# A gated two-layer transformer kernel on one Trainium2 core: block loads two blocks ahead, constants spread over later units, the next stage's first tiles loaded early

## The reference, cut to what matters

```python
x = x + tanh(g_xattn[0]) * L0_xattn(layernorm(x), ctx)       # first stage
xq   = act_fake_quant(layernorm(x))                          # one scale for the tensor
gate = xq @ weight_fake_quant(w_gate).T                      # 512 -> 1408
up   = xq @ weight_fake_quant(w_up).T
h    = act_fake_quant(silu(gate) * up)                       # scale: the largest |h| of all
x = x + tanh(g_ffn[0]) * h @ weight_fake_quant(w_down).T     # gate, up: second stage; down: third
x = x + tanh(g_xattn[1]) * L1_xattn(layernorm(x), ctx)       # third stage
x = x + tanh(g_ffn[1]) * L1_ffn(layernorm(x))                # ternary weights, third stage
```

## Time and profile before

| | |
|---|---|
| median of 3 runs | 1998.06 us (1998.03 to 2000.37) |
| the profiled execution's own time | 1998.16 us |
| its span in the trace | 1996.4 us |
| granted TensorE clock, mean | 0.972 of full speed |
| busy share: PE, DVE, ACT, POOL | 80%, 87%, 74%, 31% |
| stage two (first row product to `b_done`) | about 971 to 1176 us |
| stage three | about 1176 us to the end |

### The profile page before, as it was taken

One profiled execution on the slowest core, in us unless ns is written; L12 is line 12 of the kernel. 1 busy time (PEld: TensorE's weight loads), 2 busy tenths in 40 slices (PEclk: granted clock), 3 DMA queues, 4 the chain that ended last, 5 costly groups with the idle time before them and its releaser, 6 DMA issues.

```text
span 1996.4 us, 24448 instructions
## 1 busy us (share of the span) xinstructions
PE 1607.0 (80%) x9510; PEld 719.2 (36%) x9510; DVE 1744.6 (87%) x2619; ACT 1485.4 (74%) x1098; POOL 616.0 (31%) x480
## 2 busy tenths in 40 slices
PE   6868965697658966785598969999999987888886
PEld 3212211132112211231243435666666643334432
DVE  6899998999999988898577767999999669999997
ACT  4899999999999999999253745555454357767771
POOL 1000000000000000000161226666666545887882
PEclk9999999999999999999799989999999988999999
DMA  5000200020000010000485753333332111432312
GB/s 198 1 8 30 69 11 1 22 74 22 1 1 1 22 53 1 1 11 1 157 315 215 257 174 123 106 101 108 112 107 84 43 35 32 72 55 76 63 43 74
DMA packets 116709, 143.65 MB, mean 72 GB/s; under 512 B 25326, under 2 KB 74606, under 8 KB 116210
## 3 DMA queue, kind: packets, MB, share of 16 engines
q1 hardware_dynamic: 116594, 142.10, 22.8%
HBM read 87.55 MB, written 50.33 MB: 69 GB/s over the span
## 4 chain that ended last, share of the span: by engine, by line
ACT 42%; PE 29%; DVE 18%; issue 4%; DMA 3%; POOL 3%; SPq 0%; DVEq 0%; POOLq 0%; ACTq 0%
ACT unit L514 39%; PE psum L1645 5%; PE psum L1679 5%; PE psum L1631 3%; DVE hmax_parts L1427 3%; DVE psum L1416 3%; PE psum L1009 3%; PE psum L1015 3%; DVE unit L423 2%; PE psum L1655 2%; DMA xblk<-xnT_scratch 2%; PE psum L1672 2%; PE psum L1664 1%; POOL hidden L1835 1%; PE psum L547 1%
## 5 line engine op out<-in xcount | busy, mean ns | idle before, releaser
L514 ACT ACTIVATE unit<-unit 128x4096 f32<-128x4096 f32 x244 | 857.5, 3615 | 0.5 <-DVE unit L423 0.3
L423 DVE TENSOR_SCALAR unit<-feat_proj,text_proj 128x1024 f32<-128x1024 f32 x976 | 667.3, 746 | 67.2 <-PE psum L639 65.4
L639 PE MATMUL psum<-unit,w_pad 128*32 128x512 f32 x3904 | 474.4, 604 | 234.1 <-ACT unit L514 234.1
L639 PEld LDWEIGHTS psum<-unit,w_pad 128*32 128x32 f32 x3904 | 102.5, 110 | 556.7 <-ACT unit L514 398.2
L680 POOL TENSOR_SCALAR red<-red 128x8 f32<-128x8 f32 x4 | 2.0, 509 | 531.5 <-DVE red L321 531.5
L1818 POOL TENSOR_TENSOR h<-h,arow 128x512 f32<-128x512 f32 x104 | 135.7, 1318 | 72.1 <-ACT h L1580 71.7
L1697 PE MATMUL psum<-xq_block,w_q 128*128 128x512 bf16 x512 | 125.7, 391 | 25.4 <-ACT hidden L1599 21.0
L680 POOL TENSOR_SCALAR rstd<-mv 128x8 f32<-128x8 f32 (+1 forms) x5 | 1.7, 336 | 411.4 <-DVE mv L216 411.4
L547 PE MATMUL psum<-xnT,W_sb 128*128 128x512 f32 x256 | 125.2, 617 | 2.1 <-ACT xnT L465 2.1
L1587 ACT ACTIVATE psum<-h,conv_b_sb,conv_w_sb 128x512 f32<-128x512 f32 x112 | 86.2, 779 | 53.4 <-POOL h L1818 46.6
L1732 PE MATMUL psum<-w_q,hidden_q 128*128 128x512 fp8e4 x448 | 101.3, 379 | 21.1 <-ACT hidden_q L1610 10.8
(11 more groups left out here) (255 smaller groups left out, 2756.8 us busy)
## 6 DMA issues: line engine op xcount, KB each, us to landing
h_scratch<-h SPq DMA_DIRECT2D x44, 512.0 KB, 3.5
hin<-h_scratch SPq DMA_DIRECT2D x32, 704.0 KB, 4.7
xin<-in_x SPq DMA_DIRECT2D x8, 1024.0 KB, 6.7
tern_in<-in_w1T SPq DMA_DIRECT2D x16, 512.0 KB, 5.4
tern_in<-in_w2T SPq DMA_DIRECT2D x16, 512.0 KB, 5.4
x<-in_x SPq DMA_DIRECT2D x16, 512.0 KB, 3.6
x_scratch<-x SPq DMA_DIRECT2D x32, 256.0 KB, 2.0
x3in<-x_scratch SPq DMA_DIRECT2D x31, 256.0 KB, 3.1
```

Source lines behind the costliest of these rows:

```text
L423: ins = ve.tensor_scalar(units[:, n % 3, k, :], FP[:, bi % 2, k, :], TP[:, k, n:n + 1], None, ALU.add)
L514: ac.activation(units[:, n % 3], units[:, n % 3], ACT.Tanh).then_inc(unit_tanh, 1)
L639: mm = te.matmul(psum[k * TG:(k + 1) * TG, 3 + 2 * grp + half, :], w_pad[:, k, TG - 1 - tt:2 * TG - 1 - tt], units[:, n % 3, k, half * BAN ...
```

## The change

It changes when SyncE issues four kinds of load in stage two, the order of TensorE's first six half products, when VectorE makes the mask, and what opens stage three:

- The half blocks of the third and fourth block are loaded right behind the unit that rounds the buffer's old content two blocks earlier, in units 5 and 9 of block `o` for block `o + 2` (units 5, 9, 16 and 20, in place of 13, 17, 24 and 28).
- The seven constants are loaded one by one in units 18 to 24, and the mask and `bo_row` are made in unit 28.
- In unit 36 SyncE loads the first two tiles of `hin` and the first group of `x`, ahead of the store of that unit. `hin` and `x2` were moved in SBUF for this (behind `scores`).
- TensorE starts with the products of the first half of the first block: gate 0, up 0, gate 1, then the same three for the second half.
- ScalarE goes into stage three on `hscale_step` 5 (the reciprocal of the scale) and waits for `b_done` only before the second tile. VectorE scales `bq` and copies the keys behind the clip of the second tile (slot 315) in place of ahead of everything.

```diff
+    PREFETCH_SLOT = 36
+    CONST_SLOT, MASK_SLOT = 18, 28
...
-            if n == 10:
+            if n == MASK_SLOT:
                 V.wait_ge(const_c_loaded, NCONST_C)
...
+        def product(pair, w, n, half):
+            o, i = divmod(n, NI)
+            T.wait_ge(xq_step, 3 * (2 * o + half + 1))
+            for k in range(KC):
+                mm = te.matmul(pair[:, half, :], w[:, k, i * P:(i + 1) * P],
+                               xqT[:, o % 2, k, half * BLK:(half + 1) * BLK], start=(k == 0), stop=(k == KC - 1))
+            return mm
+
+        for half in range(2):
+            mm = product(gate_pair(0), wgT, 0, half)
...
+            mm = product(up_pair(0), wuT, 0, half)
...
+            mm = product(gate_pair(1), wgT, 1, half)
...
         for n in range(NH):
             o, i = divmod(n, NI)
...
+            if n > 1:
+                T.wait_ge(h_done, 2 * (n - 2) + 1)
+                product(gate_pair(n), wgT, n, 0)
+                product(gate_pair(n), wgT, n, 1).then_inc(gate_mm, 1)
+            if n > 0:
+                T.wait_ge(silu_done, n)
+                product(up_pair(n), wuT, n, 0)
+                product(up_pair(n), wuT, n, 1).then_inc(up_mm, 1)
...
             for half in range(2):
-                if 1 <= o < NB - 1 and i == ROUND_SLOT[half] - 2:
-                    load_block(o + 1, half)
+                if o + 2 < NB and i == ROUND_SLOT[half] + 1:
+                    load_block(o + 2, half)
             for r in range(2, KC):
                 if n == NI * (r - 1):
                     load_down(r)
+            if CONST_SLOT <= n < CONST_SLOT + len(consts):
+                sp.dma_start(*consts[n - CONST_SLOT]).then_inc(const_c_loaded, 16)
+            if n == PREFETCH_SLOT:
+                S.wait_ge(xq_step, 6 * NB)
+                stored = NI * (ORDER.index(0) + 1) - 1
+                for q in range(HR):
+                    S.wait_ge(h_stored[q], 16 * ((stored - q) // HR + 1))
+                for t in range(2):
+                    sp.dma_start(hin[:, t], h_dram[0][:, :, t * P:(t + 1) * P]).then_inc(hin_loaded[t], 16)
+                sp.dma_start(x2[:, 0:TPG, :], x[0:GRP, :].rearrange("(i p) d -> p i d", p=P)).then_inc(x2_loaded[0], 16)
             S.wait_ge(h_done, 2 * n + 1)
...
+    KEYS_AT = HQ2[1] + 1
...
+            if q == KEYS_AT:
+                ve.tensor_scalar(bq_s[:, :], bq_sb[:, :], INV_SQRT_HD, None, ALU.mult).then_inc(kd_copied, 1)
+                V.wait_ge(edges_done, 1)
...
     def scalar_C():
-        A.wait_ge(b_done, 1)
+        A.wait_ge(hscale_step, 5)
...
             for g, i, t in at1(q, SHIFT):
+                if t == 1:
+                    A.wait_ge(b_done, 1)
```

More of the change, by code:

```diff
@@ L1002, in tensor_B @@
         T.wait_ge(kv_copied, KC + NB)
+        def product(pair, w, n, half):
[7 more added lines that the diff above has]
+            mm = product(gate_pair(0), wgT, 0, half)
+            if half == 1:
+                mm.then_inc(gate_mm, 1)
+            mm = product(up_pair(0), wuT, 0, half)
+            if half == 1:
+                mm.then_inc(up_mm, 1)
+            mm = product(gate_pair(1), wgT, 1, half)
+            if half == 1:
+                mm.then_inc(gate_mm, 1)
         for n in range(NH):
             o, i = divmod(n, NI)
[L1005 to L1017, removed]
+            if n > 1:
[6 more added lines that the diff above has]
+                product(up_pair(n), wuT, n, 1).then_inc(up_mm, 1)
             for half in range(2):
@@ L1083, in sync_B @@
         load_down(1)
[L1084 to L1087, removed]
+        consts = ((bq_sb[:, :], bq), (bo_row[:, :], bo.broadcast_to([P, D])), (cw_sb[:, :, :], conv_w),
+                  (cb_sb[:, :], conv_b), (km_u8[:, :, :], kmask.rearrange("(t p) k -> p t k", p=P)),
+                  (wq_sb[:, :, :], WqT), (wo_sb[:, :, :], WoT))
         for n in range(NH):
@@ L1126, in flamingo @@
     pc = ExitStack()
-    hin = sb("hin", [P, 2, NI, P], stack=pc)
     hq = sb("hq", [P, 2, NI, P], BF16, stack=pc)
@@ L1132, in flamingo @@
     qT = sb("qT", [P, KC, GRP], stack=pc)
+    sc = sb("scores", [P, 2, HEADS, TXT], stack=pc)
+    hin = sb("hin", [P, 2, NI, P], stack=pc)
     X2R = 8
@@ L1136, in flamingo @@
     kbd = sb("k_diag", [P, NB, KC, 2 * TXT], stack=pc)
-    sc = sb("scores", [P, 2, HEADS, TXT], stack=pc)
     pT = sb("probT", [P, 2, PAIRS, P], stack=pc)
@@ L1318, in vector_C @@
     def vector_C():
[L1319 to L1325, removed]
         steps = [0]
@@ L1347, in attention @@
                 ve.tensor_scalar(hq[:, i], hq[:, i], -QMAX - 1.0, None, ALU.max).then_inc(hq_done, 1)
+            if q == KEYS_AT:
+                ve.tensor_scalar(bq_s[:, :], bq_sb[:, :], INV_SQRT_HD, None, ALU.mult).then_inc(kd_copied, 1)
+                V.wait_ge(edges_done, 1)
+                for h in range(HPC):
+                    rows = slice(h * HD, (h + 1) * HD)
+                    ins = ve.tensor_copy(kbd[rows, :, :, (h % 2) * TXT:(h % 2 + 1) * TXT],
+                                         kT[rows, :, :].rearrange("p m (b k) -> p b m k", b=NB))
+                ins.then_inc(kd_copied, 1)
             for g, i, t in at1(q, DSC):
@@ L1858, in attention @@
             for g, i, t in at1(q, X2LOAD):
-                load_x(g)
+                if g > 0:
+                    load_x(g)
             for g, i, t in at1(q, HQ2):
@@ L1915, in feed_forward @@
                     load_rows(t + 2)
-        for t in range(2):
-            load_tile(t)
         for q in range(min(0, X2LOAD[0]), QEND):
```

## The result

The changed kernel takes 1984.44 us (median of four runs, 1981.02 to 1985.88), beside 1998.32 us for the kernel before (1998.03 to 2000.37). The ratio is 0.9924, with a 95% interval of 0.9911 to 0.9936: 14 us less. The profiled execution was the fastest of the four, 1981.02 us with a span of 1979.2.

A forecast was written before the change was run, and what follows sets the result against it. The prediction took TensorE as the bound in stage three and, where undisturbed, in stage two, whose gaps could be won; its terms summed to -20.3 us, 1977.8 us from the median of 1998.06, range 1971 to 1985.

The forecast's parts named there:

- my own forecast: Whole kernel: the case that the summed terms hold, 1974 to 1982 us, chance 0.55.
- the tighter engines: Rival: VectorE or ScalarE becomes the bound of stage two, 1982 to 1991 us, chance 0.17.
- (a): Start of stage two: first products by halves let up 1 start earlier, -2.7 us.
- (b): Unit 16: the earlier load removes VectorE's wait in unit 13 and TensorE's gap, -8.7 us.
- (c): Unit 17: VectorE's wait for its half block goes, shortening TensorE's stall at the sum, -1.7 us.
- (d): Unit 31: VectorE's wait in unit 28 goes, and TensorE's gap with it, -6.6 us.
- (e): Units 18 to 28: constants loaded later and the mask moved cost almost nothing, +0.1 us.
- (f): Units 36 to 40: early tiles and `x` delay the last ternary part, so TensorE idles at unit 40, +5.3 us.
- (g): Start of stage three: earlier shift, rounding and clip bring tile 2 forward, -6.0 us.
- the part in time: Rival: the last ternary part is not held up by the early tiles, -25.6 us, 1972.5 us, chance 0.23.
- The slower case: Rival: half products leave TensorE at 1.2 GHz; lost from some six units, 2011.8 us at ten, chance 0.02.

The follow-up runs named there:

- e1: The changed kernel run again with no edit: 1986.90 us, ratio 0.9933 to the kernel before.
- e7: The kernel of e2 with TensorE's first products whole again, in the old order (gate 0, up 0, gate 1, up 1): 1979.14 us.
- e2: The changed kernel with the early loads of `hin` and `x` in unit 37 in place of 36: 1976.05 us.
- e6: The kernel of e2 with the seven constants issued at the start again and the mask made in unit 10: 1974.89 us.
- e10: The kernel of e2 with the mask made in unit 32 in place of 28: 1974.69 us.
- e4: The changed kernel with `bq` and the keys ahead of VectorE's first rounding in stage three, as before: 1987.59 us.
- e8: The kernel of e2 with the mask in unit 32, VectorE's weight sum one unit later and TensorE's product for it in unit 22: 1972.48 us.
- e9: The kernel of e8 with the constants issued at the start and the mask made in unit 10: 1970.13 us.
- e3: The changed kernel without early tiles, `hin` and the first `x` loaded behind `b_done` as before: 1982.02 us.

## Why the prediction was right, and where it was off

The forecast of 1977.8 us had the right mechanisms, but it is 6.6 us too low. The measured 1984.4 lies within the range of 1971 to 1985 by 0.6 us only, e1's 1986.9 lies outside, and neither lies in the 1974 to 1982 that I gave my own forecast. That the first number fell inside is partly luck. It falls where I had put the tighter engines (1982 to 1991), but of that case the traces show only 0.8 to 1.2 us in units 31 and 32. The largest part of the miss is the stall of the early tiles, which I had placed rightly and priced too low. Stage two was to lose 14.3 us and lost 12.8 in the first trace and 7.9 in e1.

- *(a) First products, -2.7*: up 1 starts 16.2 us behind L666 in place of 18.5, so -2.3; between e7 and e2 it is 2.0. Right.
- *(b), (c), (d) The waits for `xblk`, -8.7, -1.7, -6.6*: all four waits are gone. From L666 to gate 40 the kernel before takes 185.6 us and the changed one 167.2, 18.4 less where (a) to (e) say 19.6. In e1 it is 169.9, the difference being mostly slow groups behind the sum (1.6 us), the second gap behind the mask (0.3) and a wait for silu (0.4). Undone on e2 the loads cost 21.9, more than 17.0; a part of the excess is the new gap of 1.63 us. Right, but for the sign that TensorE would have no gap in unit 31 and no new one in units 28 to 33: there are 0.8 to 1.2 us in all.
- *(e) The constants, +0.1*: mis-sized. TensorE's gap behind the mask was 0.80 us, in e1 0.88 and 0.32, and without the mask there (e6, e10) it is gone. I took VectorE's lag to stay just inside what TensorE allows. The mask took 1.16 us there and the clip behind it 1.58 for the usual 1.22, because GpSimd was clipping the ternary parts (timelines of GpSimd and VectorE):

```profile
1101.97 1.04 POOL L1063 TENSOR_SCALAR tern_in<-tern_in 128x1024 f32<-128x1024 f32 x1 [1.94 <-ACT tern_in L958]
1105.51 1.04 POOL L1063 TENSOR_SCALAR tern_in<-tern_in 128x1024 f32<-128x1024 f32 x1 [2.50 <-ACT tern_in L958]
...
1102.13 1.16 DVE L897 TENSOR_SCALAR neg_mask<-km_u 128x512 f32<-128x512 uint8 x1
1106.05 1.58 DVE L836 TENSOR_SCALAR xblk<-xblk 128x2048 f32<-128x2048 f32 x1
```

  Where no instruction of GpSimd has begun before it, the mask takes 0.42 us (e1, e2, e10); the 0.93 that I took for its price was itself stretched by an instruction of GpSimd. This is not what makes the gap: in e1 the mask took 0.42 and the gap was 0.88.
- *(f) The early tiles, +5.3*: the right place (unit 40), the right chain and the right sign, shown by e2; ScalarE waits 5.44 us and TensorE 4.32, as the prediction asked for. The term is what failed in size: the first trace has 4.32 + 1.34 = 5.7 us, but e1 has 8.0, and the medians of e1 and e2 differ by 10.9. I priced the slow groups at 1.6 from one gap; they cost between 1.3 and 3.1. I also had SyncE issuing on time ("the issues fit ahead of the `h` of unit 36") and the part waiting in the queue. In the trace most of the delay is SyncE itself: against gate 39 the part goes out 5.1 us later than before, and the two held issues take 4.7 us over their usual time. The Trainium skill ("DMA: Bandwidth & Descriptors", Bandwidth, Measured) has two figures for a 1 MB load that lead to different estimates: its 341 GB/s gives the 5.7 us of the prediction for tiles and `x`, its 6.15 us gives about 11.5. The trace has 11.2 us from the issue of the first tile (1126.50) to the landing of `x`, 8.6 us behind its issue, with other transfers under way and 324 GB/s in all between 1126 and 1138. So the smaller stall that I took from the rate is not borne out.
- *(g) The boundary, -6.0*: -5.2 in the first trace, -5.0 in e1. The first clip ends 3.4 us behind the start of L926 as forecast (3.5). Off was the load of tile 2, which took 5.5 us and not 4.7. The load of tile 3 now follows 1.4 us behind it, but that this is why isn't shown: before, tile 0 landed in 4.6 us with tile 1 0.6 us behind. The keys fitted, and e4 shows about 3.5 us for their move, of the 3 I named.
- Stage three behind the q products came out 1.0 us longer (2.4 in e1). I had taken it as unchanged.

Against the forecast the first trace, whose execution is the fastest of its four, lacks 3.1 us: 1.5 in stage two, 0.8 at the boundary and 1.0 behind, less 0.2 ahead of stage two. e1's trace lacks 9.6: to these come 2.3 us more of stall in unit 40, 1.6 us of slow groups at the sum, about a microsecond of small gaps and 1.4 us in stage three.

Of the rivals, the part in time did not occur in the change, and e2 shows what it would have been: 1976, where I had 1972.5; beside the kernel before on its own chip that is 23.8 us less for my 25.6. The slower case needed six units at 1.2 GHz; among the gate and up products of the traces no slow stretch is longer than about three groups.

## What to carry to other kernels

A load that is issued early because its destination is free still takes its place in a queue: ask which small, urgent transfer stands behind it, and issue it right after the last one of these (one unit later was worth 10.9 us here, where the whole change had brought 12.9 on the same chip). Load a buffer as soon as its old content is used up; with two blocks of distance four waits of 14.5 us in all vanish. And do not put a one-off piece of work into the unit that already carries the most on that engine: moving the sum to a quieter unit took 5.2 us off stage two and 2.2 off the median (e8 beside e10). Repeat the unedited kernel before you price small differences: here its stage two differed by 4.9 us between two traces.

## What the runs showed of the hardware

- An issue on SyncE can itself be held. With three large loads in a row, behind others, that of 0.5 MB of `x` took 3.74 us (4.02 in e1, 4.82 in e2), while the issue of a ternary part of the same size takes 0.3 to 0.4. What holds it, these runs do not show.
- The same gap costs different amounts in different executions. Behind 3.6 us of idle at the sum, the slow groups cost 1.3 us in one trace (granted clock 0.55, then 1.00) and 2.9 in another (0.50, then 0.57). With the groups behind unit 40 this is 3.4 of the 6.5 us between the two traces of the changed kernel. The last versions, e8 and e9, have no gap over a microsecond between the first products and the end of the up products, and their runs agree within 0.8 us; but the five runs of e1, with two long gaps, agree within 1.0, so the gaps do not explain the spread by themselves.
- VectorE stands while GpSimd finishes. An instruction of VectorE on 128 x 4 elements takes 0.25 us in the changed kernel and 1.85 beside GpSimd's clear (e4). The clip of a half block takes 1.22 us; where a clip of GpSimd's had begun 0.2 to 0.5 us before it, it took 1.58 (changed), 1.91 (e1 and e7) and 1.81 (e3), and in all four it ended 1.08 us behind GpSimd's. The Trainium skill ("SBUF — State Buffer", Who interferes with whom) describes the port pair that the two share as an exclusive lock. The traces agree: VectorE does nearly all of its work after GpSimd's instruction, and not at a lower rate beside it.
